# First attention: a weight row taken off, its place in the states used for the biases

## What is computed

```python
x = L0_attn_states                                   # (4, 1024, 128)
h = (x - mean(x)) / sqrt(var(x) + 1e-5)              # over the features
q, k, v = (tanh(h @ W + bias) for (Wq, bq), (Wk, bk), (Wv, bv))   # W: (128, 1024)
alpha = softmax(where(causal, q @ k.T / 8, lowest))  # per head
ctx = alpha @ v
x = x + layernorm(tanh(ctx @ Wo + bo))
x = x + layernorm(ffn(layernorm(x)))                 # unchanged here
```

## Time and profile before

| | |
|---|---|
| median of 3 runs | 1804.86 us (1802.99 to 1805.49) |
| the profiled execution, own time | 1805.83 us |
| its span (first to last recorded instruction) | 1803.8 us |
| PE busy | 1644.7 us, 91% |
| DVE busy | 1438.8 us, 80% |
| ACT busy | 1223.1 us, 68% |
| POOL busy | 373.7 us, 21% |
| L508 to L511, matmuls | 4 x 256 of 128 x 128 |

### The profile page before, as it was taken

One profiled execution on the slowest core, in us unless ns is written; L12 is line 12 of the kernel. 1 busy time (PEld: TensorE's weight loads), 2 busy tenths in 40 slices (PEclk: granted clock), 3 DMA queues, 4 the chain that ended last, 5 costly groups with the idle time before them and its releaser, 6 DMA issues. The chain is left out here.

```text
span 1803.8 us, 39594 instructions
## 1 busy us (share of the span) xinstructions
PE 1644.7 (91%) x14930; PEld 714.7 (40%) x14930; DVE 1438.8 (80%) x2115; ACT 1223.1 (68%) x1186; POOL 373.7 (21%) x505
## 2 busy tenths in 40 slices
PE   1499999999999999994999999999999999889995
PEld 1244444444444444442223233322232332366774
DVE  5067777888888888887898899897988999367888
ACT  4276666666666666652687778786777788756776
POOL 5011111333333333332321000100010212130004
PEclk8699999999999999995799899998999999979998
DMA  4311101100000000001101100110011010000001
GB/s 109 88 37 38 37 36 37 38 36 36 36 36 36 36 35 36 20 4 31 54 25 34 26 14 25 35 26 15 24 28 33 13 36 13 1 14 13 13 12 47
DMA packets 48154, 57.13 MB, mean 32 GB/s; under 512 B 9406, under 2 KB 34462, under 8 KB 48032
## 3 DMA queue, kind: packets, MB, share of 16 engines
q1 hardware_dynamic: 45920, 51.62, 9.2%
q10 hardware_dynamic: 2112, 3.86, 1.0%
HBM read 15.07 MB, written 10.49 MB: 14 GB/s over the span
## 5 line engine op out<-in xcount | busy, mean ns | idle before, releaser
L1464 DVE TENSOR_REDUCE arena<-psum 128x2 f32<-128x1024 f32 x490 | 581.5, 1219 | 62.0 <-PE psum L1113 57.7
L1290 ACT ACTIVATE arena<-psum 128x1024 f32<-128x1024 f32 x512 | 523.4, 1025 | 157.2 <-PE psum L1083 143.2
L642 ACT ACTIVATE arena<-psum 128x2048 f32<-128x2048 f32 (+1 forms) x160 | 273.4, 1708 | 232.6 <-PE psum L527 229.9
L1098 PE MATMUL psum<-arena 128*32 128x256 f32 x4096 | 337.2, 401 | 1.6 <-ACT arena L1304 0.7
L697 POOL TENSOR_SCALAR_AFFINE_SELECT arena<-arena 128x512 f32<-128x512 f32 (+1 forms) x160 | 167.9, 1067 | 571.3 <-ACT arena L642 571.3
L544 PE MATMUL psum<-arena,hs 128*64 128x512 f32 (+3 forms) x1536 | 283.0, 496 | 2.7 <-POOL arena L697 2.2
L1113 PE MATMUL psum<-arena 32*128 32x512 bf16 x1068 | 211.9, 412 | 25.1 <-ACT arena L1343 11.8
L527 PE MATMUL psum<-arena 64*128 64x512 f16 (+3 forms) x2304 | 216.3, 325 | 4.9 <-DVE arena L732 3.6
L1083 PE MATMUL psum<-arena 32*128 32x512 bf16 x1024 | 203.8, 395 | 4.5 <-issue 3.1
L732 DVE TENSOR_TENSOR arena<-arena 128x1024 f16<-128x1024 f32 x64 | 78.4, 1225 | 162.1 <-ACT arena L621 162.1
L544 PEld LDWEIGHTS psum<-arena,hs 128*64 128x64 f32 x1536 | 96.1, 136 | 144.8 <-issue 125.9
(11 more groups left out here) (202 smaller groups left out, 2115.5 us busy)
## 6 DMA issues: line engine op xcount, KB each, us to landing
arena<-arena SPq DMA_DIRECT2D x32, 512.0 KB, 3.0
arena<-arena SPq DMA_DIRECT2D x48, 128.0 KB, 2.3
arena<-latent_q SPq DMA_DIRECT2D x64, 64.0 KB, 1.9
arena<-latent_k SPq DMA_DIRECT2D x64, 64.0 KB, 2.0
arena<-arena SPq DMA_DIRECT2D x32, 96.0 KB, 2.6
X<-in_L_attn_states SPq DMA_DIRECT2D x4, 512.0 KB, 14.0
arena<-arena SPq DMA_DIRECT2D x32, 64.0 KB, 1.8
out_x<-X SPq DMA_DIRECT2D x4, 512.0 KB, 3.2
```

What stands on the lines that cost most here:

```text
L642: nc.scalar.activation(probs[g], SC[:, :, 0:WIDTH[g]], ACT.Exp, scale=DH ** -0.5).then_inc(exp_done, 1)
L1098: last = nc.tensor.matmul(OT[ROWS * c:ROWS * (c + 1), h * HALF // 2:(h + 1) * HALF // 2], v_cols[par][:, kt, 2 * pr + i, :], e_probs[u % 4 ...
L1290: nc.scalar.activation(e_probs[u % 4], src, ACT.Exp, scale=KD ** -0.5).then_inc(e_done, 1)
L1464: nc.vector.tensor_reduce(half_tops[:, kh, qt, 2 * pr:2 * pr + 2], src.rearrange("p (i c) -> p i c", i=2), AX.X, ALU.max).then_inc(top_don ...
```

## The change

Normalized states have a mean of zero over the 128 features, so a constant taken off a column of a weight matrix does not change the product. The change takes each weight's first row off all of its rows. Row 0 is then zero, and entry 0 of the normalized states is not needed. That entry is set to 1 (`hs[:, :, 0:1]`), and row 0 of each weight holds the bias.

In setup, the first rows of the three weights are loaded apart (`w_first`), spread over the partitions by PE with a row `others` (0 for row 0, 1 for the other 127) into PSUM banks 0 to 5, and taken off `w_in` by DVE (`w_less`). The weights are loaded as rows 1 to 127, and the bias goes to row 0. DVE's wait and subtractions stand after the statistics of batch 0. In the attention, the fourth matmul of `values`, `pick_bias`, the third value slot, `qk_bias` and the bias of `tanh` are gone.

```diff
-QSLOT, KSLOT, VSLOT, OSLOT, NSLOT = 0, 2, 4, 7, 9
+QSLOT, KSLOT, VSLOT, OSLOT, NSLOT = 0, 2, 4, 6, 8
...
                 for t, w in enumerate((Wq, Wk, Wv)):
-                    act.dma_start(w_in[:, t, :], w).then_inc(w_got, 16)
-                act.wait_ge(consts, 4)
-                for t, w in enumerate((bq, bk)):
-                    act.dma_start(bias_in[0:PAIRS, t, :], w.rearrange("(n c) -> n c", n=PAIRS)).then_inc(b_got, 16)
-                for row in (0, 32):
-                    act.dma_start(vbias[row:row + 1, :], bv.rearrange("(a n) -> a n", a=1)).then_inc(b_got, 16)
+                    act.dma_start(w_first[0:1, t, :], w[0:1, :]).then_inc(first_got, 16)
+                for t, (w, bias) in enumerate(((Wq, bq), (Wk, bk), (Wv, bv))):
+                    act.dma_start(w_in[1:P, t, :], w[1:P, :]).then_inc(w_got, 16)
+                    act.dma_start(w_in[0:1, t, :], bias.rearrange("(a n) -> a n", a=1)).then_inc(w_got, 16)
...
-                act.wait_ge(w_got, 48)
                 for t, slot in enumerate((QSLOT, KSLOT, VSLOT)):
+                    act.wait_ge(w_less, t + 1)
                     nc.scalar.activation(W_all[:, :, slot, :], w_in[:, t, :].rearrange("p (n c) -> p n c", n=PAIRS),
                                          ACT.Copy, scale=WSCALE).then_inc(whi_done, 1)
-                act.wait_ge(b_got, 64)
-                nc.scalar.activation(vb_hi[0:64, :], vbias[0:64, :], ACT.Copy, scale=WSCALE).then_inc(whi_done, 1)
...
-                        last = nc.scalar.activation(hs[:, t, :], X[:, t, :], ACT.Identity, scale=rstd[:, t:t + 1],
+                        last = nc.scalar.activation(hs[:, t, 1:], X[:, t, 1:], ACT.Identity, scale=rstd[:, t:t + 1],
                                                     bias=shift0[:, t:t + 1])
...
-                nc.scalar.copy(qk_bias, bank(0)[:, 0:2 * PAIRS].rearrange("p (t n) -> p t n", t=2)).then_inc(a0s, 1)
...
-                nc.gpsimd.memset(vbias, 0.0).then_inc(consts, 1)
-                nc.gpsimd.memset(bias_in, 0.0).then_inc(consts, 1)
+                nc.gpsimd.memset(hs[:, :, 0:1], 1.0).then_inc(consts, 1)
...
                     norm_stats(dve, steps, lambda t: X[:, b * T + t, :], b).then_inc(mv0, 1)
+                    if b == 0:
+                        dve.wait_ge(w_got, 16 * 6)
+                        for t in range(3):
+                            dve.wait_ge(first_spread, t + 1)
+                            nc.vector.tensor_tensor(w_in[:, t, :], w_in[:, t, :], bank(2 * t, 2), ALU.subtract
+                                                    ).then_inc(w_less, 1)
...
-                steps.done(nc.vector.memset(W_all[:, :, VSLOT + 2, :], 0.0))
-                steps.now()
-                rows = vb_hi.rearrange("p (n c) -> p n c", n=PAIRS)
-                nc.vector.tensor_copy(W_all[0:32, :, VSLOT + 2, :], rows[0:32]).then_inc(wlo_done, 1)
-                nc.vector.scalar_tensor_tensor(
-                    W_all[32:64, :, VSLOT + 2, :], vbias[32:64, :].rearrange("p (n c) -> p n c", n=PAIRS), WSCALE,
-                    rows[32:64], ALU.mult, ALU.subtract).then_inc(wlo_done, 1)
...
+                pe.wait_ge(others_set, 2)
+                pe.wait_ge(first_got, 48)
+                for t in range(3):
+                    for half in range(2):
+                        last = nc.tensor.matmul(bank(2 * t + half), others[0:1, :],
+                                                w_first[0:1, t, half * HALF:(half + 1) * HALF], start=True, stop=True)
+                    last.then_inc(first_spread, 1)
...
-                        nc.tensor.matmul(o, xT[par][:, 1, tok], w_v[par][:, 0, :], start=False, stop=False)
-                        last = nc.tensor.matmul(o, pick_bias, w_v[par][:, 2, :], start=False, stop=True)
+                        last = nc.tensor.matmul(o, xT[par][:, 1, tok], w_v[par][:, 0, :], start=False, stop=True)
...
-                    nc.scalar.activation(qk_hi[par][j], PJ, ACT.Tanh, scale=1.0 / WSCALE, bias=bias).then_inc(tanh_done, 1)
+                    nc.scalar.activation(qk_hi[par][j], PJ, ACT.Tanh, scale=1.0 / WSCALE).then_inc(tanh_done, 1)
```

More of the change, by code:

```diff
@@ L161, in build @@
         wo_in0 = a0.take(PAIRS * D).rearrange("p (n d) -> p n d", n=PAIRS)
-        bias_in = a0.take(2 * P).rearrange("p (t n) -> p t n", t=2)
-        vbias = a0.take(H1 * DH)
-        vb_hi = a0.take(H1 * DH // 2, F16)
+        w_first = a0.take(3 * H1 * DH).rearrange("p (t n) -> p t n", t=3)
+        others = a0.take(P)
         shift0 = a0.take(NT)
@@ L169, in build @@
         wo_got, wo_split = sem("wo_got"), sem("wo_split")
-        small_in, w_got, b_got = sem("small_in"), sem("w_got"), sem("b_got")
+        small_in, w_got, first_got = sem("small_in"), sem("w_got"), sem("first_got")
+        others_set, first_spread, w_less = sem("others_set"), sem("first_spread"), sem("w_less")
         consts0, consts = sem("consts0"), sem("consts")
@@ L284, in _ @@
                 steps = Steps(dve, d0)
-                steps.done(nc.vector.memset(pick_bias, 0.0))
-                steps.now()
-                for row in (0, 32):
-                    steps.done(nc.vector.memset(pick_bias[row:row + 1, :], 1.0))
+                nc.vector.memset(others[0:1, 0:1], 0.0).then_inc(others_set, 1)
+                nc.vector.memset(others[0:1, 1:], 1.0).then_inc(others_set, 1)
                 for e in range(E):
@@ L297, in _ @@
                     for t in range(b * T, (b + 1) * T):
-                        last = nc.vector.tensor_scalar(hs[:, t, :], X[:, t, :], mv[:, t, 0:1], rstd[:, t:t + 1],
+                        last = nc.vector.tensor_scalar(hs[:, t, 1:], X[:, t, 1:], mv[:, t, 0:1], rstd[:, t:t + 1],
                                                        ALU.subtract, ALU.mult)
                     last.then_inc(xn0, 1)
-                dve.wait_ge(w_got, 48)
-                dve.wait_ge(whi_done, 4)
+                dve.wait_ge(whi_done, 3)
                 for t, slot in enumerate((QSLOT, KSLOT, VSLOT)):
@@ L331, in _ @@
                     last.then_inc(xt_ps, 1)
-                pe.wait_ge(b_got, 64)
                 pe.wait_ge(xt_lo, 1)
-                for t in range(2):
-                    last = nc.tensor.transpose(bank(0)[:, t * PAIRS:(t + 1) * PAIRS], bias_in[0:PAIRS, t, :],
-                                               ident[0:PAIRS, 0:PAIRS])
                 pe.wait_ge(small_in, 16 * SMALL)
-                at = 2 * PAIRS + E * FC
-                nc.tensor.transpose(bank(0)[:, 2 * PAIRS:at], b1_in[0:E * FC, :], ident[0:E * FC, 0:E * FC])
+                at = E * FC
+                nc.tensor.transpose(bank(0)[:, 0:at], b1_in[0:E * FC, :], ident[0:E * FC, 0:E * FC])
                 last = nc.tensor.transpose(bank(0)[:, at:at + 1], b_lat_in[:, :], ident[0:1, 0:1])
@@ L345, in build @@
         w_qk = [a1b.take(4 * P // 2, F16).rearrange("p (j c) -> p j c", j=4) for _ in range(2)]
-        w_v = [a1b.take(3 * P // 2, F16).rearrange("p (j c) -> p j c", j=3) for _ in range(2)]
+        w_v = [a1b.take(2 * P // 2, F16).rearrange("p (j c) -> p j c", j=2) for _ in range(2)]
         w_o = [a1b.take(2 * D // 2, F16).rearrange("p (j d) -> p j d", j=2) for _ in range(2)]
```

19 lines of the change are left out of this document (9 added, 10 removed).

## The result

The changed kernel takes 1838.6 us in the median (1835.7 to 1840.0), beside 1803.9 us for the kernel before; the ratio is 1.020, with an interval of 1.016 to 1.024. Timed once more beside the kernel before (experiment 5) it is 1840.3 against 1796.6 us, ratio 1.024, 1.021 to 1.028. One of experiment 8's six executions took 2548.6 us at a mean clock of 0.55; the median in the table has it (1782.2 us without it), the ratio doesn't. The prediction was 1857 us with 1847 to 1868: slower, as said, by a mechanism that the trace confirms nearly to the number, but by less than said.

A forecast was written before the change was run, and what follows sets the result against it. TensorE's instruction stream was taken to bound the attention, and a chain from X's landing the setup. Setup +66.5 us and loop -14.7 gave +51.8 on a span of 1803.8, about 1857 us after correction to the median; range 1847 to 1868.

The forecast's parts named there:

- the base: Whole program: the profiled span of the kernel before, 1803.8 us, with nothing changing behind the loop.
- the gain of the loop: Attention loop: 256 fewer `pick_bias` matmuls, 0.056 us each (0.106 in the first pair), save 14.7 us, lower bound 9.6.
- the clock: Setup: PE, idle for 70 us and more, runs its transposes at clock 0.50, adding 3 us, bounds 0 and 4.
- The transfer: Setup: 127-row weight loads run on one DMA engine, so weights are complete at 74.7 us, bounds 67 and 83.
- the queue behind the wait: Setup: the chain from batch 1's statistics to the barrier starts at 78.4 us and keeps its 25.7 us.
- The subtractions: Setup: three DVE subtractions of 128 x 1024 fp32 take 1.22 us each, 3.7 us, after the weights arrive.
- the transposes of before had 1.00 for 24 of 32: Setup of the kernel before: 24 of PE's 32 transposes were taken to run at full granted clock, 0.233 us each.
- the tanh is the same instruction: Attention loop: dropping the bias from the tanh of queries and keys brings no gain that can be placed.
- Rival 1: Setup: the 127 rows are dealt over many engines, weights arrive at some 11 us, total 1790 us, faster; 8%.
- break-even at about 5 engines: Setup: the loop's gain pays the loss if weights come before 26 us, needing about 5 or more engines.
- Rival 2: Setup: one engine alone is slower per packet, 0.297 us, so 48 us more, 1905 us; 4%.
- Rival 3: Attention loop: it keeps its length because PE waits for DVE's addition into `acc`, 1871 us; 2%.

The follow-up runs named there:

- experiment 5: The changed kernel without further edit, timed again beside the kernel before in the same rounds: 1840.3 against 1796.6 us, ratio 1.024.
- experiment 8: The kernel before without the 256 `pick_bias` matmuls in `values`, leaving out the bias of the values: 1783.4 us, ratio 0.993.
- experiment 9: The kernel before without the bias operand on the tanh of queries and keys, all matmuls kept: 1791.7 us, ratio 0.997.

## Why the prediction was right or wrong

The direction and the mechanism were right. The time fell below the range because three terms of the sum were off, all to the same side: the base by 10.6 us, the gain of the loop by 7.7 and the clock by 3.

**The transfer** was right. One engine, weights at 74.7 us forecast and 74.42 measured; the 1 us allowed for the signal doesn't show (the last packet began at 74.41), and the packets took 0.7 us longer in all. The price per packet, 0.171 us and that divided by 1.07, is 0.160, and the row shows 0.156 once X has landed. The queue behind the wait was also right: 25.7 us from batch 1's statistics to the barrier, 25.6 measured (77.82 to 103.42). The subtractions took 3.48 us, forecast 3.7, and PE's spreading of the first rows (10.6 us for three weights) was over long before, as argued.

**The clock term** was wrong, 3 us, and so was the reading of rows 8 that it rests on. The sum let the transposes run at 1.00 in the kernel before and at 0.50 in the changed one. The first trace's clock records begin only at 29.3 us, the changed kernel's at 90.0, and ahead of its first record the view of windows shows 1.00. What the clock was there is to be read from the distance of two transposes' starts. It is 0.213 us from 23.87 us on in the kernel before, 0.213 from 86.77 us on in the changed kernel, 0.213 where the recorded clock is 0.50 (eight transposes at 834 us before), and 0.109 where it is recorded as 1.00. Eight transposes in the changed kernel's first execution, where 0.50 is recorded, in its second, where 1.00 is, and in the kernel before at 834 us:

```profile
95.39 1.97 PE L327 MATMUL psum<-ident,hs 128*128 128x128 f32 x8 [4.06 <-ACT hs L220]
```
```profile
95.36 1.09 PE L327 MATMUL psum<-ident,hs 128*128 128x128 f32 x8 [2.94 <-ACT hs L220]
```
```profile
834.10 1.94 PE L1064 MATMUL psum<-ident,hs 128*128 128x128 f32 x8 [3.63 <-PEq L449]
```

So the changed kernel's transposes began at the slow pace, as forecast, but those of before had done so too, 24 in 5.60 us, and there was nothing to add: from batch 1's statistics to the barrier it is 25.7 us before and 25.6 after. The step that failed is "the transposes of before had 1.00 for 24 of 32".

**The loop's gain** was too small. The term was 14.7 us, 13.9 for 31 pairs and 0.85 for the first. Four of the 32 `values` stand ahead of the first addition, so 2.2 us of the term (0.85 and 3 x 0.45) belong there and 12.5 to the 31 intervals between additions. These gave 12.0 for the matmuls (experiment 8), about as forecast, but 18.4 in all. The step that failed is the sentence "the tanh is the same instruction": it has one operand less, and 3.8 us hang on that (experiment 9). The last 2 to 2.5 us of the loop's gain stay open. I had called the normed pairs bound by PE because PE was at 97 to 99% busy; but the 0.19 us by which PE waits for DVE's addition in each was the sign that DVE's addition comes last there, and ahead of it ACT's time can count as PE's does. From the barrier to the first addition it was another 4.0 us less, of which 2.2 were in the sum; the remaining 1.8 are less than the 2.1 us by which two executions of the changed kernel differ there, so they aren't a measured effect.

**The base** was taken too surely. The sum put the span at 1855.6 us and it was 1833.6. Of the 22.0 us, 3.7 are the setup (3 of it the clock), 7.7 the stretch from the barrier to the last addition (22.4 for 14.7) and 10.6 the second half, which no line of the change touches. So the term of the sum that was off by most is its base, the span of 1803.8 us: it holds 973.3 us for the second half, which took 962.7 in the changed kernel's execution and varies without any edit. The profile of before came from an execution with a mean clock of 0.93 there, and the kernel's three runs (1803.0 to 1805.5) agreed so well that no spread was put into the range for it. A fourth took 1793.8, and over the later sessions it ran from 1791 to 1815 us, with medians of 1797 to 1801. With setup and loop alone, +62.8 - 22.4 = 40.4 us on 1797 would be 1837. The size of the change, +51.8 us in the sum, was 43.7 when both kernels were timed side by side (experiment 5).

**The rivals.** Rival 1 (many engines) is out for ACT's queue by the 6.2%, but it is what happens when GpSimd issues the same copy, and its time, 1790 us, would have been 1779 to 1780 beside the lower base. Its break-even at about 5 engines was near: with 4 engines and the weights at 28 us the kernel is level with before (0.998, 0.995 to 1.001), the loop's gain being larger than the 14.7 us with which it was worked out. Rival 2 (slow single engine) is out by 0.156 us a packet. Rival 3 (the gain is given back) is out: the pairs got shorter by all of it and more.

## What to carry to other kernels

Taking one row off a 128-row copy is not a small edit: on ScalarE's queue 127 rows ran at a sixteenth of the rate, 124 at a quarter, and the next wait stood for 60 us. Read the share of 16 engines of a queue with a backlog, and when a slice is odd, cut it in pieces whose rows have a large divisor up to 16 (15 + 112 here), or let GpSimd issue it. And when a loop mixes kinds of iterations, read the length of each kind: a small wait of the bounding engine marks those in which another engine's nanoseconds can count too. And before a clock is read from a window near the start of a trace, compare the distance of like instructions there with a place where the clock is on record.

## What the runs showed of the hardware

- ScalarE's queue moved 127 rows of 4 KB with 6.2% of the 16 DMA engines, and 124 rows with 26%; GpSimd's queue moved the 127 with 64%.
- One engine alone moved 4 KB in 0.156 us, no slower than each of 16 side by side (0.171 us).
- A tanh of 128 x 1024 out of PSUM takes 1.11 to 1.12 us with a bias per partition and 1.02 to 1.03 us without (experiment 9; 1.03 to 1.05 in the changed kernel).
- Transposes of 128 x 128 fp32 start 0.109 us apart where the clock is recorded as 1.00 and 0.213 us apart where it is recorded as 0.50. In all 13 traces they start 0.213 us apart ahead of the first clock record, where the view shows 1.00; PE had done nothing for 24 us (before) or 70 us (changed kernel) before these transposes.
- The unchanged second half took 960.7 us (experiment 8) to 973.3 us in different executions, with a mean clock of 0.95 and 0.93. Why one execution gets more time at half clock than another stays open.
- Six fp32 matmuls of one row by 512 columns took 10.6 us of PE (12 records, 0.853 us apart), ahead of the first clock record; fp32 matmuls with 512 columns are 0.853 us apart at a recorded 0.50 too (from 837.7 us in the kernel before).
